# One expert-weight load issued ahead of the combine table's store, the second half's turn of q and k three slots later, and the output projections one slot later, in a two-layer attention and expert kernel

## The reference, cut to what matters

```python
    xn = _layernorm(x, axis=-1)
    s = _L1_attn_ref(xn, ...)     # q, k, v; rmsnorm of q and k; softmax; values; projection by w_proj
    g = _silu(_L1_ffn_ref(xn, ...))
    x = x + s * g

# in _L1_ffn_ref
    topk_w, topk_idx = jax.lax.top_k(probs, TOP_K)
    combine = combine.at[jnp.arange(T)[:, None], topk_idx].add(topk_w)
    def expert_step(acc, ws):
        gw, uw, dw, ce = ws
        out = jax.nn.silu(x @ gw) * (x @ uw) @ dw
        return (acc + ce[:, None].astype(out.dtype) * out, None)
```

## Time and profile before

| | us |
|---|---|
| median of 3 runs (1396.48 to 1396.93) | 1396.88 |
| the profiled execution, its own time | 1398.46 |
| its span | 1396.7 |
| TensorE busy in the span | 1352.6 (97%) |
| VectorE busy | 906.8 (65%) |
| ScalarE busy | 756.2 (54%) |
| GpSimd busy | 727.8 (52%) |

### The profile page before, as it was taken

How to read it: one execution, slowest core, us unless ns; L and a number is a source line. 1 busy time by engine, 2 the same in 40 slices (tenths; PEclk the granted TensorE clock), 3 DMA queues, 4 the chain that set the end, 5 groups by cost and what they waited for, 6 DMA issues and landing times. The chain is left out here.

```text
span 1396.7 us, 25325 instructions
## 1 busy us (share of the span) xinstructions
PE 1352.6 (97%) x8758; PEld 1205.1 (86%) x8758; DVE 906.8 (65%) x1807; ACT 756.2 (54%) x1964; POOL 727.8 (52%) x719
## 2 busy tenths in 40 slices
PE   8999899999999999999999999889999999999998
PEld 7887798999899989998998898768889888888897
DVE  6655566566656665666565665557887778786765
ACT  4553454445544555455545444246666666666664
POOL 1651343445343555344635453447657676766775
PEclk9999999999999999999999999999999999999999
DMA  5995333224422353234324424266555663645662
GB/s 185 318 337 202 84 91 97 84 77 120 113 82 49 103 144 85 62 91 114 97 63 120 118 63 127 95 189 186 162 169 156 197 176 112 205 138 181 177 194 91
DMA packets 105646, 190.51 MB, mean 136 GB/s; under 512 B 20433, under 2 KB 39569, under 8 KB 103217
## 3 DMA queue, kind: packets, MB, share of 16 engines
q1 hardware_dynamic: 105520, 188.91, 45.5%
HBM read 116.41 MB, written 30.47 MB: 105 GB/s over the span
## 5 line engine op out<-in xcount | busy, mean ns | idle before, releaser
L776 POOL TENSOR_TENSOR a_pr<-a_pr,a_ri 128x512 f32<-128x512 f32 x128 | 133.4, 1042 | 299.9 <-DVE a_ri L956 299.9
L833 ACT ACTIVATE a_pr<-a_score,a_nb 128x256 f32<-128x256 f32 x256 | 119.2, 471 | 267.7 <-DVE a_nb L948 267.7
L1374 POOL TENSOR_TENSOR l_pr<-l_pr,l_ri 128x512 f32<-128x512 f32 x128 | 133.3, 1042 | 126.4 <-DVE l_ri L1730 125.2
L1489 ACT ACTIVATE l_pr<-l_score,l_nb 128x256 f32<-128x256 f32 x256 | 119.3, 472 | 100.7 <-DVE l_nb L1699 100.7
L58 PE MATMUL a_job<-s_xs,s_wh 128*128 128x512 f32 x384 | 153.6, 400 | 1.0 <-PEq L222 1.0
L60 PE MATMUL a_job<-s_xs,s_wl 128*128 128x512 f32 x384 | 152.1, 396 | 0.0
L59 PE MATMUL a_job<-s_xs,s_wh 128*128 128x512 f32 x384 | 151.4, 394 | 0.0
L948 DVE TENSOR_REDUCE a_nb<-a_score 128x2 f32<-128x512 f32 x128 | 88.5, 692 | 86.1 <-PE a_score L1027 84.2
L1699 DVE TENSOR_REDUCE l_nb<-l_score 128x2 f32<-128x512 f32 x128 | 87.5, 684 | 32.1 <-PE l_score L1838 31.9
L961 DVE TENSOR_TENSOR a_pt<-a_turn,a_pt 128x512 fp32r<-128x512 f32 x128 | 87.5, 684 | 23.8 <-ACT a_pt L841 23.8
L58 PE MATMUL l_job<-l_xs,s_wl 128*128 128x512 f32 x224 | 90.3, 403 | 5.9 <-DMA s_wl<-wgu_scratch 5.8
(11 more groups left out here) (252 smaller groups left out, 4565.4 us busy)
## 6 DMA issues: line engine op xcount, KB each, us to landing
s_wl<-wgu_scratch SPq DMA_DIRECT2D x56, 512.0 KB, 5.7
a_sk<-a_rotk SPq DMA_DIRECT2D x384, 64.0 KB, 2.0
a_sq<-a_rotq SPq DMA_DIRECT2D x256, 64.0 KB, 2.0
s_xs<-xn_scratch SPq DMA_DIRECT2D x14, 1024.0 KB, 5.6
l_wd<-wd_scratch SPq DMA_DIRECT2D x56, 256.0 KB, 2.9
l_zq<-qs_scratch SPq DMA_DIRECT2D x128, 64.0 KB, 4.3
l_sk<-ks_scratch SPq DMA_DIRECT2D x32, 256.0 KB, 4.7
a_raw<-in_w SPq DMA_DIRECT2D x30, 256.0 KB, 2.9
```

The source lines that it names most:

```text
L776: pool.tensor_tensor(e, e, ri[:, n % 2, :].unsqueeze(2).broadcast_to([P, 2, SEQ]), ALU.mult)\
L833: i = act.activation(pr[:, n % 2, t, :], PS[n % 2][:, t * SEQ:(t + 1) * SEQ], ACT.Exp, bias=nb[:, n % 2, t:t + 1], accum_out=sm[:, n % 2, ...
L1374: pool.tensor_tensor(e, e, ri[:, n % 3, :].unsqueeze(2).broadcast_to([P, 2, SEQ]), ALU.mult)\
L1489: i = act.activation(pr[:, n % 3, t, :], PS[n % NPS][:, t * SEQ:(t + 1) * SEQ], ACT.Exp, bias=nb[:, n % 3, t:t + 1], accum_out=sm[:, n % 3 ...
```

## The change

Three edits, all in `stage_layer1`:

```diff
     def X_AT(m):
-        return (8, 9) if m == 0 else (9, 10)
+        return (8, 9) if m == 0 else (9, 13)
@@ attn_jobs
-        if u in (3, 4) and b >= 1:
-            jobs.append((f"P{u - 3}", b - 1))
+        first = 3 if b == BATCH else 4
+        if u in (first, first + 1) and b >= 1:
+            jobs.append((f"P{u - first}", b - 1))
@@ SyncE
                 for K in range(L + 1):
-                    if 2 <= K < L:
+                    s, k = step_of(K)
+                    first_combine = k == NSH + 1 and s == 0
+                    if 2 <= K < L and not (k == NSH + 2 and s == 0):
                         stack_until(AT["U", K - NGU] if K >= NGU else SLOTS[0])
                         load_gu(K)
                     if K >= 1:
                         stack_until(AT["D1", K - 1 - ND] if K > ND else SLOTS[0])
                         load_d(K - 1)
-                    s, k = step_of(K)
+                    if first_combine:
+                        load_gu(K + 1)
                     if k == NSH + 1 and s < NSTEP:
                         stack_until(AT["C", s])
                         store_combine(s)
```

## The result

| | us |
|---|---|
| before, median of 20 runs (1395.72 to 1402.71) | 1397.43 |
| after, median of 20 runs (1399.40 to 1403.84) | 1401.22 |
| ratio, with its 95% interval | 1.0027 (1.0021 to 1.0033) |
| span of the profiled execution, before and after | 1396.7, 1400.2 |

The change makes the kernel slower, by 0.27%, some 3.8 us. The span grew by 3.5 us, so the profile can account for it.

What follows compares the result with a forecast made beforehand. TensorE, busy 97% of the span, was taken as the bound; the edits could only move excess. Load +0.2, projections +2.9 and `X1` -1.6 made +1.5 us, from 1396.88 to about 1398.4 us, range 1393.6 to 1402.4.

Steps and rivals of the forecast that it cites:

- slower rival: Emptied slots 22, 54 and 86: VectorE's lateness is paid in full, 5.0 to 6.9 us; total +5.4, 1402.3 us; chance 0.19.
- first edit: Tile 5's weight load issued earlier: TensorE's 5.8 us wait becomes some 6 us for GpSimd; +0.2 us, from -3.1 to +1.0.
- emptied slots: Slots 19 to 23, 51 to 55, 83 to 87: position left empty by moved projections; +2.9 us, range +1.5 to +5.0.
- batches 2, 4 and 6: Projections change place with expert items of the same price in full slots: 0, give or take 0.8 us.
- `X1`: `X1` moved to position 13: less excess at positions 10 to 12, a new wait at 14; -1.6 us, range 0 to -4.0.
- ring-order rival: All 512 KB of the load come before the store: 1.2 us more on the first edit, 1399.6 us; chance 0.10.
- The rival's condition: The slower rival decides once VectorE is over 0.4 us late at slot 22's scores; it was 0.45 late before.
- The sign that I gave for batch 2: In the changed kernel's profile, slots 42 to 44 show under 1 us of excess, and slot 46 more than before.
- faster rival: Spread rows land earlier and the first pair of edits works: -3.1, -4.0 and +2.0 make -5.1, 1391.8 us; chance 0.14.
- third edit: Output projections moved, leaving slots 22, 54 and 86 emptied: +2.9 us in the forecast, +2.0 in the faster rival.

## Why the prediction was right in its range and wrong in its likeliest case

**The whole.** The median of 1401.22 lies in the range, 2.8 us above the forecast; 0.55 us of this is that before, too, has a higher median over 20 runs (1397.43) than over the three that I started from. The likeliest case was no change and it came out slower by more than 0.2%. It is not the slower rival as I put it either: its size is nearly met (1402.3), but its first edit came to -0.2 instead of +1.0 and its emptied slots to 4.1 instead of 5.0 to 6.9. In the profile the 2.0 us between the forecast's +1.5 and the measured +3.5 are +1.2 in the emptied slots, +2.0 in batches 2, 4 and 6, -0.4 for the load and -0.9 for `X1`. So part of it is luck: a gain of `X1` that I had too small hid almost half of a loss that I had at nothing.

**The load edit: right in its mechanism, and close partly by luck.** I had the wait of 5.8 us replaced by one of 6 for GpSimd, with the same reason: 5.78 us at line 1762. The delay of the chain was too small: I had 0.7 us, 0.3 of it for the DMA engines, and the edit made it 1.1, 0.6 of it there. SyncE's head start of 0.4 us, and spread rows that took 0.4 us less, made up for it. `D0` was forecast at 933.6 and came at 933.16, slot 0 at 934.9 and came at 934.61. The longer low clock is there too, 0.66 where it had been 0.93. My upper end of +1.0 was too low by its own terms, since `D0` at 934.4 and the full 1.0 us of low clock make +1.4. I missed the wait for the stack's `l_sk`, 0.65 us in front of slot -1's scores. The load is issued ahead of it: all seven kernels with that order wait there, 0.31 to 1.30 us, and none of the seven others does. The ring-order rival would have made the chain 1.2 us later than I had it, and it was 0.4 earlier. The Trainium skill, "DMA: Bandwidth & Descriptors", section "Queues, rings and completion order", has the descriptors of one issuing engine consumed in ring order on each DMA engine. The trace agrees as far as it goes: the load landed 4.5 us after its issue, at 923.9, and the store's wait ended after that, at 925.2. The cost to the store was 0.6 us and not the 1.5 us that I let this rule add. A likely reason is that the load had been issued 3 us ahead of the store and was largely through by then; no run tests it, and landing in this order does not prove the rule.

**The emptied slots: right mechanism, undersized.** Slots 22 and 23 were forecast at 5.8 to 6.2 us and lasted 6.23; slots 19 to 23 at 17.7 to 18.6 and lasted 18.44. What was mis-sized is my choice in the middle of this and "the same or a little less" for the other two places: they lost 1.35 and 1.13 us, together 4.1 where I took 2.9. The rival's condition (VectorE late at slot 22's scores) was not met: line 1703 started 0.48 us after the scores, so VectorE was in time, as "slot 20 lets it catch up" had it. The slots are long even so: from slot 22's maximum to slot 23's VectorE works for 3.40 us without a wait (1011.69 to 1015.09), and the slot lasts 2.84. Of this, line 1707 to the reciprocal took 2.72 us where I had kept the 2.32 of before; 0.25 of the 0.40 us is the operation of 32 columns that GpSimd's held (0.49 instead of 0.24).

**Batches 2, 4 and 6: the step that failed.** "In batches 2, 4 and 6 the projections change place with expert items of the same price in full slots: 0, give or take 0.8." It measured +0.6, -0.3 and +1.1 in the change, with +0.6 more in slots 41 and 42, together +2.0, and alone +2.1 at the same slots. The price that I compared was TensorE's. On VectorE the two are not the same: in front of slot 36's maximum stood `P0`'s line 1586 with 0.4 us, and now stands the gating of `G` with 0.69, which waits for ScalarE too. Why slots 41 and 42 grow stays open. In batch 4 slot 68 loses 0.3 us in this way, and slots 70 and 72 give back more.

**`X1`: right mechanism, undersized.** I took -1.6. It gave -2.5 in the change, and alone -2.5 by slots and -2.9 (-4.2 to -1.7) by the ratio. Position 10 keeps its excess as forecast (2.9 us over batches 0 to 6, forecast 3.0), and positions 11 and 12 keep 2.2 (forecast 1.6). At positions 13 and 14 the excess grew by 2.0 where I had added 2.9: position 14 had 0.9 us before, which I had not taken off. The sign that I gave for batch 2, under 1 us of excess in slots 42 to 44, was missed: it is 1.4 us, nearly all in slot 42.

**The faster rival.** It asked for spread rows that land earlier. With the load in front of the stack they don't; with the store in front of it they do, and with `X1` moved the whole comes near the rival's 1391.8 us, though without the third edit, for which the rival had +2.0.

## What to carry to other kernels

When a wait is taken away, follow the next operation's own chain to its first issue before moving anything: here two waits ended within 2 us of each other, and only the version that moved the later chain's root (a store of 16 KB, whose flight could lie beside other issues) gained. When items change places, compare what they cost on every engine and on which side of the pacing operation they fall, not only on the engine that is busy. A slot left without work on the bound engine is only free if the others have none in it either.

## What the runs showed of the hardware

**VectorE and GpSimd hold each other up.** The row of line 1663 above is one case. In the kernel with the shortened sum, line 1629's copy of 32 columns takes 0.17 us when GpSimd is idle. Under a running GpSimd operation it, or the operation behind it, ended within 0.06 us of GpSimd's end each of the six times, and was 0.70 to 1.32 us long. GpSimd waits in its turn: its line 1386 above took 1.73 us beside line 1601, and 1.26 to 1.36 us the 55 other times that it runs in this layer.

The sum of squares that it replaces is not held: 1.05 to 1.18 us with or without GpSimd beside it. The Trainium skill, "SBUF — State Buffer", section "Who interferes with whom", describes a port pair that the two engines lock for a whole instruction, which a reduction never takes, and the trace agrees. So one cannot price a short VectorE operation by its columns alone where GpSimd is busy as much as here.

**The clock drops in some executions and not in others, with the same work.** The stretch from 900 to 908 us comes ahead of every edit. The first two rows are of before and the last two of after:

```profile
900.00:904.00 4.00, 4.00 (x27) 3.81 (x27) 3.43 (x12) 0.59 (x2) 2.82 (x6) 0.77 0.00 0
904.00:908.00 4.00, 4.00 (x16) 3.21 (x15) 3.62 (x13) 1.40 (x3) 3.37 (x11) 0.80 0.01 2
```

```profile
900.00:904.00 4.00, 4.00 (x30) 3.74 (x30) 3.43 (x12) 0.72 (x2) 2.81 (x6) 1.00 0.00 0
904.00:908.00 4.00, 3.64 (x16) 2.67 (x15) 3.62 (x13) 1.27 (x2) 3.39 (x10) 1.00 0.38 117
```

In kernels that are the same up to slot 4 (`X1` alone, the projections alone, even or odd batches alone), slot 4 began 0.8 to 2.2 us earlier than in the profile of before. That is as much as the effects looked for, and why the experiments are read from slot 4 on. Behind it two places vary with the same items: slot 14 lasts 3.25 us in the profile of before and 3.6 to 4.0 in six others that have `X1` of this batch at position 10, and in front of slot 71's scores the wait for the stack is 0.16 us in before and 0.6 to 1.2 in eight others, which slot 72 gives back. Where the projections of batch 4 are moved, there is no such wait.
